# One core: the output projection of a recurrent block, made per unit of 512 tokens, with stores in runs of four rows

## The reference

```
s = attention(xn) @ wo.T + bo        # 16 heads; each query samples k and v at 12 positions,
                                     # linearly interpolated between neighbouring tokens,
                                     # softmax over the 12 scores
f = mixture of experts(xn)           # 8 experts, top 2 by router score; per expert
                                     # silu(a) * b, hidden width 512, then back to 256
out = x + s * silu(f)
```

## Time and profile before

| | |
|---|---|
| Median of 3 runs | 1524.09 us (1520.70 to 1526.34) |
| The profiled execution | 1524.51 us |
| Its span, first to last instruction | 1522.9 us |
| Granted TensorE clock, mean | 0.967 |
| Busy share of the span | PE 91%, PEld 73%, DVE 87%, ACT 54%, POOL 44% |
| Last stage | about 1240 us to the end |

### The profile page before, as it was taken

How to read it: one execution, slowest core, us unless ns; L and a number is a source line. 1 busy time by engine, 2 the same in 40 slices (tenths; PEclk the granted TensorE clock), 3 DMA queues, 4 the chain that set the end, 5 groups by cost and what they waited for, 6 DMA issues and landing times.

```text
span 1522.9 us, 36336 instructions
## 1 busy us (share of the span) xinstructions
PE 1380.8 (91%) x13943; PEld 1107.0 (73%) x13944; DVE 1329.2 (87%) x1651; ACT 825.7 (54%) x1889; POOL 667.7 (44%) x432
## 2 busy tenths in 40 slices
PE   5998999997399999999999999999999967787988
PEld 4864666666278888888888887878888856565766
DVE  7837767767499999999999999999999999999971
ACT  2547676666265546465455545544554536565665
POOL 1001000000367777686766768777676842211011
PEclk9998999999699999999999999999999989898999
DMA  7934655656756767767676766757676768999998
GB/s 224 348 129 96 164 138 162 173 139 175 249 159 170 224 180 216 212 181 226 155 231 155 230 181 165 211 144 209 159 230 176 176 160 223 257 203 238 239 239 157
DMA packets 200861, 293.35 MB, mean 193 GB/s; under 512 B 22242, under 2 KB 157670, under 8 KB 200500
## 3 DMA queue, kind: packets, MB, share of 16 engines
q0 software_dynamic: 61536, 146.37, 37.2%
q1 hardware_dynamic: 137731, 144.88, 34.0%
q10 hardware_dynamic: 1488, 0.80, 0.2%
HBM read 182.75 MB, written 117.60 MB: 197 GB/s over the span
## 4 chain that ended last, share of the span: by engine, by line
DVE 53%; issue 7%; PE 6%; DMA 5%; SPq 2%; ACT 0%; POOL 0%; DVEq 0%; ACTq 0%; POOLq 0%
DVE gslope L1664 12%; DVE parts L1660 12%; DVE parts L1620 9%; DVE expert_mem L1586 5%; DMA band<-band_rows 4%; DVE parts L1632 3%; DVE parts L1636 2%; PE pB L1491 2%; DVE parts L1639 2%; PE pA L1476 1%; SPq L1126 1%; DVE gslope L1717 1%; DVE wgt L1725 1%; DVE score L1642 1%; DVE score L1643 1%
## 5 line engine op out<-in xcount | busy, mean ns | idle before, releaser
L1184 POOL DMA_INDIRECT moe_rows<-expert_mem,token_of x142 | 349.3, 2460 | 80.1 <-issue 49.0
L1457 PE MATMUL pA<-xsT,expert_mem 128*128 128x256 f32 x1136 | 260.5, 383 | 18.8 <-ACT xsT L1287 8.5
L1463 PE MATMUL pY<-expert_mem 128*128 x1136 | 265.9, 387 | 0.0
L1457 PE MATMUL pB<-xsT,expert_mem 128*128 128x256 f32 x1136 | 256.8, 379 | 0.0
L1457 PEld LDWEIGHTS pA<-xsT,expert_mem 128*128 128x128 f32 x1136 | 217.2, 192 | 51.5 <-issue 19.2
L1463 PEld LDWEIGHTS pY<-expert_mem 128*128 128x128 f32 x1136 | 211.1, 191 | 42.3 <-issue 16.1
L1165 POOL DMA_INDIRECT expert_mem<-xn_rows,token_of x142 | 197.5, 1391 | 90.6 <-issue 82.5
L1457 PEld LDWEIGHTS pB<-xsT,expert_mem 128*128 128x128 f32 x1136 | 215.8, 190 | 29.3
L1664 DVE TENSOR_REDUCE gslope<-parts 128x256 f32<-128x3072 f32 x64 | 214.7, 3354 | 2.2
L1660 DVE SCALAR_TENSOR_TENSOR parts<-posw,prob 128x768 f32<-128x768 f32 x240 | 213.8, 953 | 1.0
L1306 ACT ACTIVATE expert_mem<-pA,b1sel 128x256 f32<-128x256 f32 x284 | 111.3, 475 | 150.7 <-DVE expert_mem L1586 66.7
(11 more groups left out here) (202 smaller groups left out, 2146.9 us busy)
## 6 DMA issues: line engine op xcount, KB each, us to landing
expert_mem<-in_w_l POOLq DMA_DIRECT2D x71, 1024.0 KB, 7.1
band<-band_rows SPq DMA_DIRECT2D x256, 96.0 KB, 5.1
S_rows<-stage SPq DMA_DIRECT2D x256, 94.0 KB, 2.0
band_rows<-wgt SPq DMA_DIRECT2D x12, 1536.0 KB, 6.9
xn_rows<-stage SPq DMA_DIRECT2D x16, 512.0 KB, 5.9
v_rows<-stage SPq DMA_DIRECT2D x16, 512.0 KB, 4.7
moe_rows<-zeros POOLq DMA_DIRECT2D x4, 2048.0 KB, 10.2
out<-in_x SPq DMA_DIRECT2D x16, 512.0 KB, 8.3
```

The source lines that it names most:

```text
L1184: nc.gpsimd.indirect_dma_start(out=dram["moe"], out_offset=bass.IndirectOffsetOnAxis(ap=keep["inv"][:, 2 * n + s:2 * n + s + 1], axis=0), ...
L1457: mm = nc.tensor.matmul(dst[:, c], w1[:, 1 - u, k, o * HID + c * P:o * HID + (c + 1) * P], xsT[:, k], start=(k == 0), stop=(k == KC - 1))
L1463: mm = nc.tensor.matmul(pY[:, s], hid[:, h, c, s * P:(s + 1) * P], w2[:, c, ds(e * D, D)], start=False, stop=(s == 1 and c == HC - 1))
```

## The change

The projection of a unit's four tiles is no longer made tile by tile. `outT` holds a whole unit of 512 tokens, twice, in memory that the expert weights had used. `project(i, h, u)` makes half a unit: the bias for two slices of 256 columns in one matmul of 512 columns, then for each slice two matmuls whose weights are every fourth token of the unit, starting at token 2h or 2h + 1. Partition p of the result so holds tokens 4p to 4p + 3, and `unit_rows` now describes a unit's rows in DRAM that way: each partition's four rows are one run of 4 KB in the load of the expert rows and in the accumulating store. TensorE projects the halves of unit i - 1 beside the first and the third tile of unit i. ScalarE copies half a unit, 512 columns, at once (`evacuate_unit`). The last unit keeps its order of rows and is made tile by tile (`project_tile`, `evacuate_tile`); before it the two halves of unit 14 stand beside its first two tiles, tiles 60 and 61 are projected beside tile 62, and tiles 62 and 63 after tile 63. There are eight slots for projected units in place of ten. TensorE's loop has the first three units written out, then six rounds of eight tiles.

```diff
-ROW_SLOTS = 10
+ROW_SLOTS = 8
...
+        outT = pool_mem[:, W2_F + LATE_F:W2_F + W1_F].rearrange("p (u c n) -> p u c n", u=2, c=KC)
+        proj = pool_mem[:, W2_F + W1_F:W2_F + W1_F + ROW_SLOTS * UNIT_F].rearrange("p (k a c) -> p k a c", k=ROW_SLOTS, a=GROUP)
...
         def unit_rows(t, k):
-            return t[k * GTOK:(k + 1) * GTOK, :].rearrange("(a p) c -> p a c", p=P)
+            rows = t[k * GTOK:(k + 1) * GTOK, :]
+            return rows.rearrange("(p a) c -> p a c", a=GROUP) if k < LAST else rows.rearrange("(a p) c -> p a c", p=P)
...
             def evacuate_out(t):
+                i, col = t // GROUP, t % GROUP * P
                 act.wait_ge(pv_done, t + 1)
-                if t >= 2:
-                    act.wait_ge(pj_done, t - 1)
+                if i >= 2:
+                    act.wait_ge(pj_done, 2 * (i - 1))
                 for c in range(KC):
-                    ins = nc.scalar.activation(outT[:, t % 2, c], pV[t % 2][:, c * P:(c + 1) * P], ACT.Identity, bias=bv[:, c:c + 1])
+                    ins = nc.scalar.activation(outT[:, i % 2, c, col:col + P], pV[t % 2][:, c * P:(c + 1) * P], ACT.Identity,
+                                               bias=bv[:, c:c + 1])
                 ins.then_inc(outT_ready, 1)
...
+            def evacuate_unit(i, h):
+
+                act.wait_ge(pj_done, 2 * i + h + 1)
...
+                if i >= ROW_SLOTS and h == 0:
+                    act.wait_ge(out_stored[i % ROW_SLOTS], 16 * (i // ROW_SLOTS))
+                nc.scalar.activation(proj[:, i % ROW_SLOTS, 2 * h:2 * h + 2], pJ[h][:], ACT.Identity).then_inc(pj_ready, 1)
...
+            for t in range(TILES):
+                if t > 0 and t + 1 < TILES:
+                    evacuate_band(t + 1, 0)
+                    evacuate_band(t + 1, 1)
+                evacuate_out(t)
+                i, j = t // GROUP, t % GROUP
+                if i > 0 and i < LAST and j % 2 == 0:
+                    evacuate_unit(i - 1, j // 2)
...
-            def project(t, u):
+            def project(i, h, u):
+
+                pe.wait_ge(outT_ready, GROUP * i + GROUP)
+                if not (isinstance(i, int) and i == 0):
+                    pe.wait_ge(pj_ready, 2 * i + h - 1)
+                nc.tensor.matmul(pJ[h][:], ones3[:], bo[:, None, :].broadcast_to([NB, 2, D]), start=True, stop=False)
+                for s in range(2):
+                    for c in range(KC):
+                        mm = nc.tensor.matmul(pJ[h][:, s], outT[:, u, c].rearrange("p (q a) -> p a q", a=GROUP)[:, 2 * h + s],
+                                              wo[:, c], start=False, stop=(s == 1 and c == KC - 1))
+                mm.then_inc(pj_done, 1)
...
                     times_v(t, j, i)
-                    if not (first and j == 0):
-                        project(t - 1, (j + 1) % 2)
+                    if not first and not last and j % 2 == 0:
+                        project(i - 1, j // 2, 1 - u)
+                    if last and j < 2:
+                        project(i - 1, j, 1 - u)
+                    if last and j >= 2:
+                        for k in range(t - 2 if j == 2 else t - 1, t if j == 2 else t + 1):
+                            project_tile(k)
...
+            four_tiles(0, 0, first=True)
+            for i in range(1, 3):
+                four_tiles(i, i % 2)
+            with pe.Fori(1, TILES // GROUP // 2 - 1) as i:
+                for u in range(2):
+                    four_tiles(i * 2 + u + 1, 1 - u)
+            four_tiles(LAST, LAST % 2, last=True)
...
             def finish_unit(k):
 
-                dve.wait_ge(pj_ready, (k + 1) * GROUP)
+                dve.wait_ge(pj_ready, 2 * k + 2)
                 dve.wait_ge(moe_ready, k + 1)
```

More of the change, by code:

```diff
@@ L943, in mix_block @@
         LATE_F = 2 * SUBS * D
-        assert W2_F == MOE_SLOTS * UNIT_F and W1_F == 2 * LATE_F and LATE_F + HID_F + ACT_F + XS_F + YS_F >= ROW_SLOTS * UNIT_F
+        assert W2_F == MOE_SLOTS * UNIT_F and W1_F == 2 * LATE_F and HID_F + ACT_F + XS_F + YS_F >= ROW_SLOTS * UNIT_F
+        assert LATE_F == 2 * KC * GTOK
         pool_mem = sb("expert_mem", [P, MOE_F + ACT_F + XS_F + YS_F])
@@ L954, in mix_block @@
         late_v = pool_mem[:, W2_F:W2_F + LATE_F].rearrange("p (u s c) -> p u s c", u=2, s=SUBS)
-        proj = pool_mem[:, W2_F + LATE_F:W2_F + LATE_F + ROW_SLOTS * UNIT_F].rearrange("p (k a c) -> p k a c", k=ROW_SLOTS, a=GROUP)
+        outT = pool_mem[:, W2_F + LATE_F:W2_F + W1_F].rearrange("p (u c n) -> p u c n", u=2, c=KC)
+        proj = pool_mem[:, W2_F + W1_F:W2_F + W1_F + ROW_SLOTS * UNIT_F].rearrange("p (k a c) -> p k a c", k=ROW_SLOTS, a=GROUP)
         wo = sb("wo", [P, KC, D])
@@ L987, in mix_block @@
         v = sb("vk", [P, 2, SUBS, D])
-        outT = sb("outT", [P, 2, KC, P])
         rel = sb("rel", [P, 1])
@@ L1000, in mix_block @@
         pV = [pB[:, 2 * u] for u in range(2)]
-        pJ = [pY[:, 0], pO[:, 0]]
+        pJ = [pY, pO]
         w1_loaded = [sem(f"w1_loaded{u}") for u in range(2)]
@@ L1422, in _ @@
                 evacuate_y(n, n % 2, n // 2)
-            for t in range(TILES + 1):
-                if t < TILES:
-                    if t > 0 and t + 1 < TILES:
-                        evacuate_band(t + 1, 0)
-                        evacuate_band(t + 1, 1)
-                    evacuate_out(t)
-                if t > 0:
-                    evacuate_proj(t - 1)
+            for t in range(TILES):
[6 more added lines that the diff above has]
+                    evacuate_unit(i - 1, j // 2)
+                if i == LAST and j < 2:
+                    evacuate_unit(i - 1, j)
+                if i == LAST and j >= 2:
+                    for k in range(t - 2 if j == 2 else t - 1, t if j == 2 else t + 1):
+                        evacuate_tile(k)
                 if t in END_EXPONENT_AT:
@@ L1494, in times_v, with project_tile @@
                 mm.then_inc(pv_done, 1)
-            def project(t, u):
+            def project(i, h, u):
[8 more added lines that the diff above has]
+                mm.then_inc(pj_done, 1)
+            def project_tile(t):
                 pe.wait_ge(outT_ready, t + 1)
-                if not (isinstance(t, int) and t < 2):
-                    pe.wait_ge(pj_ready, t - 1)
+                pe.wait_ge(pj_ready, 2 * LAST + t - LAST * GROUP - 1)
+                here = pJ[t % 2][:, 0]
+                nc.tensor.matmul(here, ones3[:], bo[:], start=True, stop=False)
                 for c in range(KC):
-                    nc.tensor.matmul(pJ[u], outT[:, u, c], wo[:, c], start=(c == 0), stop=False)
-                nc.tensor.matmul(pJ[u], ones3[:], bo[:], start=False, stop=True).then_inc(pj_done, 1)
+                    mm = nc.tensor.matmul(here, outT[:, LAST % 2, c, t % GROUP * P:(t % GROUP + 1) * P], wo[:, c],
+                                          start=False, stop=(c == KC - 1))
+                mm.then_inc(pj_done, 1)
             def products(n, h, u):
@@ L1553, in _, with four_tiles @@
             pe.wait_ge(ys_ready, SLOT_PAIRS)
-            def four_tiles(i, first=False, last=False):
+            def four_tiles(i, u, first=False, last=False):
                 for j in range(GROUP):
@@ L1561, in four_tiles @@
                     times_v(t, j, i)
-                    if not (first and j == 0):
-                        project(t - 1, (j + 1) % 2)
-            four_tiles(0, first=True)
-            with pe.Fori(1, TILES // GROUP - 1) as i:
-                four_tiles(i)
-            four_tiles(TILES // GROUP - 1, last=True)
-            project(TILES - 1, 1)
+                    if not first and not last and j % 2 == 0:
[3 more added lines that the diff above has]
+                    if last and j >= 2:
+                        for k in range(t - 2 if j == 2 else t - 1, t if j == 2 else t + 1):
+                            project_tile(k)
[6 more added lines that the diff above has]
+            four_tiles(LAST, LAST % 2, last=True)
         @block.vector
@@ L1676, in finish_tile @@
                     dve.wait_ge(moe_ready, STEPS)
-                dve.wait_ge(pj_ready, t + 1)
+                dve.wait_ge(pj_ready, 2 * LAST + t - LAST * GROUP + 1)
                 here = proj[:, LAST % ROW_SLOTS, t % GROUP]
```

13 lines of the change are left out of this document (6 added, 7 removed).

## The result

The changed kernel is slower: 1550.85 us median (1546.64 to 1553.09, 4 runs) against 1525.21 us (1520.70 to 1531.15, 4 runs), a ratio of 1.0156 with an interval of 1.0127 to 1.0184. The profiled execution took 1550.84 us, its span is 1549.2 us: 26.3 us more than the 1522.9 us of before. The prediction was 1521 us, with a range of 1511 to 1538.

A forecast was written before the change was run, and what follows sets the result against it. The last stage was taken as two halves with a lock at tile 42, VectorE's chain before, TensorE's pace and band loads after. From 1524.5 us: lock 0, switches -0.6, strided loads +1.6, DMA -3.3, slower lines -1: about 1521, range 1511 to 1538.

The forecast's parts named there:

- The lock: After tile 42 ScalarE's in-order queue holds the last exponent, needing VectorE's score; it runs at 1436.92 us and TensorE can't pass earlier.
- The lock moves by about +0.5 us: Last exponent after tile 42: shift of about +0.5 us, within -4.6 and +6, taken as 0.
- So it arrives at 1396: VectorE reaches unit 7 at 1396, 3.3 us of earlier waits counted as gone, and waits till 1400.
- Switches -0.6: TensorE after the lock: ten blocks and four single tiles take 26.1 us against 26.7 now, 0.6 us saved.
- strided loads +1.6: TensorE's weight loads at a step of four floats: 20 ns each, 5 us in all, 1.6 us after the lock.
- DMA -3.3: After the lock, loads late at three places in a store's shadow: 1.1 us off each, bounds 0 and 8.7 us.
- slower lines -1: After the lock, half of the slower lines behind the lost waits goes too: -1 us.
- strided rival: Strided weight loads set TensorE's pace, up to 148 ns each, deciding from about 55 ns: 15 us slower, 1540 us; chance 0.15.
- The tail after tile 63 keeps its order: nothing: End of the kernel after tile 63: order unchanged, so no time gained or lost.
- Loop body: TensorE's loop of eight tiles doesn't stay loaded: up to 31 us at six back edges, 1552 us; chance 0.04.
- Packets: Rival: the stores stay in 1 KB packets, the lock moves by +3 us, 1525.5 us; chance 0.08.
- The gain: Rival: stores drop towards a load's price, strided loads cost nothing, lock moves by -3.5 us: 1514 us; chance 0.25.

The follow-up runs named there:

- The kernel before with the other table: The kernel before the change, with VectorE's table moved so that each unit is taken up one entry later: 1523.75 us, ratio 0.9988.
- light queue: The kernel before and the changed kernel, both without the loads of v beyond the first four tiles: 1518.03 us and 1522.98 us.
- order-alone kernel: The changed kernel's blocks and their places, but with packed weights and each tile's rows in the old order: 1544.61 us, ratio 1.0146.
- the rows alone: The kernel before with only runs of four rows in the expert-row load and the accumulating store, result order left wrong: 1527.32 us, ratio 0.9997.
- packed and changed kernel: Packed: the changed kernel with ScalarE sorting the values so a block's weights are 128 neighbouring columns, 1548.43 us, ratio 1.0151. Changed: the change itself, 1550.85 us.

## Why the prediction was wrong, step by step

**What bounds the kernel.** The lock is real: the exponent waits for VectorE's score in the changed kernel too. But "TensorE can't pass this point earlier" was read as if the end followed the lock alone. The kernel before with the other table moves the lock by 5.3 us and the end by nothing. Lock and bands are two limits side by side.

**"The lock moves by about +0.5 us", taken as 0.** This is the step that failed, by 18 us and far outside its own bounds of -4.6 and +6. It let band waits only shrink: it gave TensorE 6.4 us of saved matmul time, and counted the waits as something that the saving meets. It didn't ask what the four-slot prefetch sees of the new order. The cover of a tile's loads is the work that lies between two points of TensorE's queue, and the projections are nearly half of it (3.8 of 8.1 us). Moving them made it 9.1 and 6.7 us. All numbers for this were in the rows: 1.27 us a projection and 3.43 us a tile give the 8.1, and a load in the chain of the earlier trace rows took 7.96 us. Unit 7 was estimated ready at 1400 and came at about 1417.7.

**"So it arrives at 1396".** Wrong too: of the waits of 1.74 and 2.88 us 3.3 us were counted as gone, and VectorE's idle time grew to 24.6. Projecting a unit late, without lumps, already makes waits of 5.3, 7.7 and 3.0 us. The slack between a unit's being ready and VectorE's taking it up was near zero at units 3, 4 and 7. A unit is ready two tiles, 6.9 us, later; the prediction laid that on unit 7 alone, as six microseconds, and took 5.4 us of hoped-for saving off at once.

**After the lock.** Switches -0.6, strided loads +1.6, DMA -3.3 and slower lines -1 make -3.3; measured were +5.3 to tile 63. Roughly 1.7 of these are waits for bands (6.9 us against 5.2), 2.3 the wait for tile 44's transposed band right behind the exponent (2.7 against 0.4), and 1.7 longer busy time of TensorE (73.0 against 71.4). With a light queue that stretch takes 74.8 us in the changed kernel against 76.8, at granted clocks of 0.96 and 0.90, so that part of those 2 us is the clock.

**TensorE's block.** 2.1 us and 20 ns a load were forecast, 2.26. It takes 2.40. With packed weights, in the order-alone kernel, the same block takes 2.15, from a bias at 1366.47:

```profile
1366.78 1.99 PE L1519 MATMUL pY<-wo,expert_mem 128*128 128x256 f32 x8
1368.62 0.60 PE L1491 MATMUL pBT<-ident,band 128*96 128x128 f32 x4
```

So the stride costs 0.25 us a block, about 30 ns a load, where 20 were taken: matmuls stand 0.26 us apart ((2.25 - 0.40) / 7) in place of 0.23 ((1.99 - 0.38) / 7). That is below the 55 ns from which the strided rival would decide, and the block is still under the old pair's 2.54: the mechanism was right and the term somewhat small.

**The stores.** 0.9 us a store was forecast, 0.7 is what the rows alone gave. The packets did become 4 KB: 7056 in place of 12816 for the same 25.17 MB. The difference, 5760, is 15 x 384, that of the stores alone. The loads of the experts' rows were in long packets already; the earlier trace rows showed it, 578 packets for 2.12 MB, and "though their rows are 1 KB too" misread it. But the worth of it was nil, where -3.3 was counted. A queue with a share of 1.00 isn't by itself what sets the time: the changed kernel has 0.83 and waits more, because its odd tiles leave less time between the issue of a load and its use. With a third of the loaded bytes and two of six issues gone as well, the same order waits only 11.4 us.

**"The tail after tile 63 keeps its order: nothing".** It costs 2.8 us. Tiles 60 and 61 are projected together beside tile 62, unit 14's multiplication stands 5.7 us ahead of tile 63's end where it had been 8.5, and the last store's issue ends 7.6 us ahead of the span's end, not 5.0. The same 2.7 us stand in the light pair (11.9 against 9.2 us from tile 63 to the end). That a shorter distance to unit 14's store makes the last one land later fits this, but it wasn't tried by itself.

**The rivals.** Strided loads: the loads went to 332 ns, the upper bound of the rows, but packed weights give back nothing of the 26 us that the runs can tell; the case missed. By the 16-byte lines of the Trainium skill, "SBUF — State Buffer", section "Door 1", the loads slow down, and the trace agrees (332 against 190 ns); what they cost behind a matmul of 256 columns is the 30 ns above. Loop body: no repeated idle "issue" at the eighth tiles, so it missed, although its 1552 us are near the measured time. A right number would have been no proof. Packets: they changed. The gain: no.

**What stays open.** One slice beside every tile (1.0098) and one tile's projection a unit late with packed weights (1.0059) aren't told apart by their intervals, and the trace with the lock 8.4 us earlier is of a run far below its kernel's median; so what stride and rows cost in that schedule stays open. How much of the 20 us is the wait itself and how much the halved clock behind it has only an estimate: seven blocks of 1.7 us more are 12 us, six projections of 1.06 us more before are 6, so some 6 us of the loss in the projections, against 15.0 us more of waiting for bands. And a fifth slot for bands, which would lengthen every tile's cover and leave the order alone, was not run.

## What to carry to other kernels

Where loads are released by one point of an engine's queue and wanted at another, add up the work that lies between the two points for every tile, and again after a change of order: equal work in lumps makes the worst tile's cover shorter, here 6.7 in place of 8.1 us, while the loads shown needed 9.1. Before counting a saving ahead of a place where engines meet, lay the change's delay on each consumer's slack there; slack of 0.2 us is none. And before relieving a full queue, ask which traffic the late loads wait behind: 163 us less engine time in GpSimd's stores brought nothing, while taking the loads of v out of SyncE's own queue brought the changed kernel down by some 27 us.

## What the hardware showed beside that

A weight load of 128 float32 columns at a step of four takes 332 ns against 190, and a matmul of 256 columns behind it still starts 0.26 us after the one before, where packed ones stand 0.23 apart: most of the longer load is hidden at the full clock. At the halved clock the eight matmuls of a block take 3.80 us strided and 3.78 packed, so there next to nothing of the stride is seen.

Sorting the values in ScalarE's copy, with neighbouring columns of PSUM written 128 floats apart into the four slices, takes 469 ns where the plain copy of 128 columns takes 364 (means over the last stage, packed and changed kernel). The totals of the two kernels don't tell which of the two ways to pay for the order is the cheaper.

Accumulating stores cost nearly the same engine time in runs of 4 KB as in runs of 1 KB, 0.7 us a store of 0.52 MB less out of the 4.2 us that the earlier trace rows give for one. A plain load of as many bytes, whose packets are already long, costs 1.6 us there.
